# One feed-forward weight load moved ahead of each output projection in a two-block transformer kernel

## The reference

```python
x = x + attn_a(layernorm(x))   # z@wq@fcq_w+fcq_b, the same for k and v; softmax(q k^T / 8) v; @ fco_w + fco_b
x = x + ffn(layernorm(x))      # gelu(h @ w1 + b1) @ w2 + b2
x = x + attn_b(layernorm(x))   # h @ w_qkv; softmax(q k^T / 8) v; @ w_proj + b_proj
x = x + ffn(layernorm(x))      # the same w1, b1, w2, b2
```

## Time and profile before

| what | us |
|---|---|
| median of 2 runs | 3466.19 (3432.43 and 3499.94) |
| profiled execution, its own time | 3393.45 |
| its span on the slowest core (core 7) | 3392.0 |
| spans of all cores | 3331.4 to 3392.0 |

### The profile page before, as it was taken

The page is one execution under the profiler, slowest core; times in us unless marked ns, Lnnn a source line. Parts: engine busy times, 40 slices in busy tenths (PEclk is TensorE's granted clock), DMA queues, the critical chain, the costliest instruction groups (busy, mean ns, idle before and its releaser), DMA issues.

```text
span 3392.0 us, 33872 instructions; the slowest of 8 cores (3331.4 to 3392.0 us)
## 1 busy us (share of the span) xinstructions
PE 2658.3 (78%) x10664; PEld 921.6 (27%) x10664; DVE 1115.2 (33%) x1554; ACT 1612.5 (48%) x1816; POOL 65.2 (2%) x122
## 2 busy tenths in 40 slices
PE   5557878687863799899747778787878764989999
PEld 1111222122221344344213322222222221434333
DVE  4543444354433021120343344443445431111100
ACT  2248989798910302301312269883989402131220
POOL 0000000000000000000000000000000000000000
PEclk8657999799987899999868889997999887999878
DMA  3000000000016624423011110001000038352331
GB/s 113 0 1 8 5 4 4 3 4 4 5 17 96 116 39 75 75 38 63 0 22 22 22 17 5 4 4 26 5 4 4 10 50 136 72 105 60 77 76 34
DMA packets 36262, 121.00 MB, mean 36 GB/s; under 512 B 7936, under 2 KB 12032, under 8 KB 26880
## 3 DMA queue, kind: packets, MB, share of 16 engines
q0 software_dynamic: 20832, 97.53, 16.8%
q1 hardware_dynamic: 12384, 12.93, 1.3%
q10 hardware_dynamic: 2880, 8.39, 0.7%
HBM read 203.50 MB, written 8.39 MB: 62 GB/s over the span
## 4 chain that ended last, share of the span: by engine, by line
PE 58%; ACT 15%; DVE 11%; DMA 6%; issue 5%; another core or an unknown queue 3%; DVEq 0%; ACTq 0%; SPq 0%; POOLq 0%; POOL 0%
ACT POOL L469 13%; PE PS_A L714 6%; PE PS_B L714 5%; PE PS_A L408 5%; DMA POOL<-w_h 4%; PE PS_A L741 3%; PE PS_E L741 3%; PE PS_B L741 3%; PE PS_D L741 3%; PE PS_C L484 3%; PE PS_D L484 3%; DVE sstat L139 2%; PE PS_C L488 2%; DVE SCR L139 2%
## 5 line engine op out<-in xcount | busy, mean ns | idle before, releaser
L469 ACT ACTIVATE POOL<-PS_A,ebias 128x1024 bf16<-128x1024 f32 x512 | 570.4, 1114 | 104.8 <-PE PS_C L488 41.2
L469 ACT ACTIVATE POOL<-PS_B,ebias 128x1024 bf16<-128x1024 f32 x512 | 570.4, 1114 | 25.6 <-PE PS_C L488 12.4
L714 PE MATMUL PS_A<-BIG,POOL 128*128 128x512 bf16 x1024 | 265.2, 406 | 158.4 <-DMA POOL<-w_h 136.5
L143 ACT ACTIVATE BIG<-PS_A,bcols 128x512 bf16<-128x512 f32 x144 | 98.9, 687 | 567.1 <-PE PS_A L714 553.0
L408 PE MATMUL PS_A<-BIG,POOL 64*128 64x512 bf16 x512 | 197.2, 385 | 98.5 <-ACT POOL L469 96.0
L714 PE MATMUL PS_B<-BIG,POOL 128*128 128x512 bf16 x1024 | 254.8, 394 | 0.0
L408 PE MATMUL PS_B<-BIG,POOL 64*128 64x512 bf16 x512 | 197.0, 385 | 60.9 <-ACT POOL L469 58.8
L484 PE MATMUL PS_C<-POOL 128*65 128x512 bf16 x512 | 214.9, 420 | 30.2 <-DVE SCR L139 30.2
L139 DVE RECIPROCAL PF<-SCR 33x512 f32<-33x512 f32 x64 | 214.1, 3345 | 69.8 <-DMA SCR<-PF 69.8
L143 ACT ACTIVATE POOL<-X 128x512 bf16<-128x512 f32 x128 | 80.6, 630 | 321.1 <-DVE X L139 202.5
L139 DVE SCALAR_TENSOR_TENSOR X<-PS_A,bcols,X 128x512 f32<-128x512 f32 x48 | 36.0, 751 | 558.3 <-PE PS_A L741 434.3
(11 more groups left out here) (148 smaller groups left out, 3097.7 us busy)
## 6 DMA issues: line engine op xcount, KB each, us to landing
POOL<-w_h POOLq DMA_DIRECT2D x64, 1024.0 KB, 8.7
POOL<-w_h POOLq DMA_DIRECT2D x2, 8192.0 KB, 58.7
X<-xT SPq DMA_DIRECT2D x4, 1024.0 KB, 21.9
X<-xT ACTq DMA_DIRECT2D x4, 1024.0 KB, 25.0
BIG<-POOL SPq DMA_DIRECT2D x64, 64.0 KB, 1.9
POOL<-wqkv_kv POOLq DMA_DIRECT2D x16, 256.0 KB, 4.3
POOL<-wqkv_q POOLq DMA_DIRECT2D x16, 256.0 KB, 3.5
yT<-X SPq DMA_DIRECT2D x16, 256.0 KB, 2.3
```

Source lines behind the costliest of these rows:

```text
L143: return p.inc(getattr(nc.scalar, name)(*a, **k), "act", 1)
L469: nc.scalar.activation(psb, PSx[:, :], AF.Exp, bias=ebias[:, c:c + 1], scale=0.125),
L714: tt = nc.tensor.matmul(PSx[:, ucoff:ucoff + 512], wg[:, dc * 512 + j * 128: dc * 512 + j * 128 + 128], BIG2[:, hoff(dc):hoff(dc) + 512], ...
```

## The change

In both attention stages, between the pair loops and the output projection, POOL now waits for everything that has been issued so far on PE, DVE, ACT, on SP's DMA semaphore and on `g16`, and then issues the load of W1's group 0 into its slot. `emit_ffn` gets the semaphore and count of that load and leaves out its own `load_w1(0, 0)` for the first quarter.

```diff
-        def emit_ffn(store_out=False):
+        def emit_ffn(store_out=False, w1pre=None):
...
                 if ts == 0:
-                    load_w1(0, 0)
+                    if w1pre is not None:
+                        w1_loads[(0, 0)] = w1pre
+                    else:
+                        load_w1(0, 0)
                     load_w1(0, 1)
...
+            p.wait(nc.gpsimd, "te")
+            p.wait(nc.gpsimd, "dve")
+            p.wait(nc.gpsimd, "act")
+            p.wait(nc.gpsimd, "s16")
+            p.wait(nc.gpsimd, "g16")
+            w1pre = ("g16", p.inc(nc.gpsimd.dma_start(
+                POOL[:, OF_W1:OF_W1 + 4096], w1_h[0]), "g16", 16))
             emit_outproj_all(BIG1, fco_h, OA_FCO, b_fco, od, os16, kv_te)
...
-            emit_ffn()
+            emit_ffn(w1pre=w1pre)
```

More of the change, by code:

```diff
@@ L1004, in build @@
         if upto >= 4:
-            emit_ffn(store_out=True)
+            emit_ffn(store_out=True, w1pre=w1pre)
             p.barrier()
```

## The result

The changed kernel is slower by 0.3%: ratio 1.003 to the kernel before, 95% interval 1.0019 to 1.0041, which is about 10 us (6 to 14) of 3393. Its median is 3380.53 us over 39 runs; that of the kernel before, now over 38 runs, is 3404.21, and not the 3466.19 of the first two. Both sets also hold runs from 3421 to 3635 us (19 of 38 before, 14 of 39 after), in which, wherever the cores are on record, those of one die or both had a lower granted clock; the ratio is made without them, the other runs have medians of 3368.2 and 3378.6, and only because of the runs left out does the slower kernel show the lower median of all. The profiled execution took 3376.91 us; its slowest core is core 1 with a span of 3375.3, granted clock 0.893, where core 7 of the profile before had 0.884.

The account below looks back on a forecast made before the run. PE was taken as the bound (78% busy), its idle time being waits for `w_h` loads queued behind W2. Two times (13.4 cost - 6.9 gain) = 13.0 us slower, 3406.5 profiled, 3479 as median; range 3425 to 3515.

Parts of the forecast that it names:

- the base of the sum: Whole kernel: 3393.45 us plus 13.0 gives 3406.5 for the profiled execution; scaled to the runs' median of 3466.19, 3479.
- The cost at the projection: At each output projection's start: PE starts 13.4 us later, between 12.2 and 17.0, behind the new load.
- The chain (wake, W1, wake, load 0): Before each projection: POOL wakes 0.6, W1 lands 8.7, POOL wakes 0.6, load 0 lands 3.5 us.
- The gain at the stage: Each feed-forward stage: group 1 starts 9.45 or 8.3 us earlier; 6.9 us is left at group 3's end.
- The give-back: Feed-forward stages: group 3 takes over group 2's stall and cold start, so 6.9 us of 9.45 is kept.
- The first (gain lost, +25): Feed-forward stages: group 1 lands as before, 1.1 us of gain is left, +25 us, 3491; chance 0.17.
- The second (load 0 doesn't wait for the landing, 4.1 us): Projection: load 0 needn't await the new load's landing, cost 4.1, gain 9.45 kept, -11 us, 3455; chance 0.15.
- The third, the clock: Projection: matmuls lack the full clock after the longer pause; wholly cold 131 us slower with the 13, 3597; chance 0.05.
- The fourth, faster by over 2%: Whole kernel: over 2% faster, needing 69 us, where waits behind the layernorm are 38 and 34 us; chance 0.03.
- The rule on a load's duration: New load: skill's 2.0 us plus bytes over 436 per ns gives 4.4 or 6.8 us; measured 8.7 was preferred.

Follow-up runs that it names:

- e2: Changed kernel with both `emit_ffn` calls made without `w1pre`, so group 0 is loaded twice; ratio 1.0109 to the kernel before the change.
- e3: Changed kernel with the new load, still ahead of the projection's loads 0 and 1, on a semaphore of its own; ratio 1.0018 to the kernel before.
- e1: Changed kernel with the new load behind the projection's loads 0 and 1, on a semaphore of its own; ratio 0.9968 to the kernel before.
- e6: Group 0's load behind the projection's loads 0 and 1, own semaphore, plus W2 in eight loads between the projection's weight loads; ratio 0.9792 to the kernel before.
- e5: Kernel before with nothing preloaded, W1's groups 0 and 1 issued ahead of W2 at each feed-forward stage's start; ratio 0.9987 to the kernel before.

## Why the prediction was right and where it was wrong

**The time was wrong, the difference right.** I forecast 3479 us with a range of 3425 to 3515 and measured were 3380.53, below it. The step that failed is "The median of the runs is 3466.19 ... the difference carries over, to 3479": the base of the sum. I took the median of two runs that lay 67.5 us apart for the kernel's time and let it outweigh the profiled execution of 3393.45. Both of these runs, 3432.43 and 3499.94, lie above every run of this kernel that the ratio rests on: those are 19, from 3355.8 to 3387.6 with a median of 3368.2, so the base was 98 us too high. With 3368.2 the same +13 gives 3381. The sum against the profiled execution, 3406.5, would still have been 26 us too high, for that execution lay 25 above the median too. The forecast of the change itself was +13 us with +5 to +20 as its own range; measured are +10 (6 to 14). That was not luck: both of its terms, cost and gain, came out one by one, as follows.

**The cost at the projection.** Forecast 13.4 us each, measured 13.9 and 13.3, and 13.7 and 13.5 in e2. The chain (wake, W1, wake, load 0) is in the trace as written. What I had not separated is which link makes it: e3 shows that the order of landing alone makes 11.3 of it, so taking away the wait on `g16`, on which I leaned, is worth only 2.3.

**The gain at the stage.** Forecast 9.45 and 8.3 at the start of group 1; the means give 8.6 and 8.2. Forecast 6.9 left after group 3; at group 4 7.2 and 6.3 are left, and at the second product 7.2 and 8.0. The give-back is the one I named: before, group 1 to group 2 took 10.3 and 9.8 us and group 2 to group 3 7.5 and 8.0; now these are 9.2 and 8.9, and 9.2 and 9.9. That the stall would move whole from group 2 to group 3 is argued from this and the timeline; no run took it away.

**The rivals.** The first (gain lost, +25) is refuted by the start of group 1 in the changed kernel and by e1, in which the gain stands alone. The second (load 0 doesn't wait for the landing, 4.1 us) is refuted by the timeline of POOL, which issues load 0 after a wait of 10.07 us for the new load, and by e3: even without the wait on the semaphore it costs 11.3. The third, the clock, is refuted by the window over the projection, 0.98, and by the projection's unchanged length (86.9 and 86.8 in A, 87.1 and 86.6 in B). Single cores differ by more, 83.2 to 90.2 us, but three of eight are near 90 in A both before and after. By the Trainium skill, page "TensorE: Matmul & The Clock Gate", section "What's actually happening", the clock has two levels and comes back to the full one after steady work; the trace agrees, behind a wait of 3.8 and one of 18.9 us alike. The fourth, faster by over 2%, is outside the ratio's interval.

**The rule on a load's duration.** By the Trainium skill's fit, page "DMA: Bandwidth & Descriptors", section "Anatomy of one DMA — SWDGE (gpsimd) path", the new load was estimated at 4.4 or 6.8 us. Measured are 10.1 in A and 8.3 in B on core 1, and 8.0 to 10.2 over all cores. The measurement decides here. By the page's estimates the change would have come to +4 or +9; the ratio's interval of 6 to 14 leaves out the first and not the second, so it is the landing times that speak against them.

## What to carry to other kernels

In this kernel the prefetch was worth what it took out of the line that the waiting engine stands in, not the wait that the profile names after it: of the ten MB in the line (W2, group 0, group 1) it moved 1 MB, and only the share of that 1 MB in the wait could go. Before a load is moved, ask which loads it is moved in front of: in e3 they landed behind it even though nobody waited for it by name. It is the large transfer that wants a place where the line is idle. In e6 most of its pieces were issued right behind a small urgent load, some ten us before the next one, and the projections were at most 1.4 us longer.

## What the runs showed of the hardware that I had not expected

A load of 1 MB issued while W2 is under way lands only after W2 and after everything else issued before it, where its median is 8.7 us. In e5 the one issued at 1090.90 took 40.1 us: W2 still needed 34.1 of them, and the load landed 6.0 after it. In the changed kernel the one issued at 1104.27 took 28.1: W2 landed after 17.0 of them, group 1 after 23.2, and this load 4.9 later. This is the row of the changed kernel:

```profile
DMA to landing us min/median/max: 28.1/28.1/28.1
```

And eight loads of 1 MB with small ones between them, issued ten us apart for the most part, kept the line at a share of 0.81 and 138 GB/s with landings of 9.4 to 16.8 us, while PE's projection was hardly longer. I had expected the urgent loads of 256 KB to suffer from that. They did land later, after 4.8 to 8.4 us with a median of 5.0 (3.4 to 4.1, median 3.5, before), but each is needed only ten us after its issue.
